# Gated cross-attention and gated feed-forward layer, one core: sums between the values of key tiles 0 and 1, probabilities of key tiles 1 and 3 in front of the values, correction and refinement in the values' slot, and a prologue that loads c and wk first

## The reference

```python
def _layernorm(x, axis=-1, eps=1e-05):
    m = jnp.mean(x, axis=axis, keepdims=True); v = jnp.var(x, axis=axis, keepdims=True)
    return (x - m) / jnp.sqrt(v + eps)
# attention: queries from the normalised x, keys and values from ctx
q = (Q @ Wq.T + bq) ...; k = (K @ Wk.T + bk) ...; v = (V @ Wv.T + bv) ...
scores = einsum('bhqd,bhkd->bhqk', q, k) * SCALE      # then key mask and causal mask
out = einsum('bhqk,bhkd->bhqd', softmax(scores), v)
x = x + tanh(g_xattn) * (out @ Wo.T + bo)
# feed-forward on the normalised x; xr, xk mix each token with the one before it
x = x + tanh(g_ffn) * (sigmoid(xr @ W_r.T) * (square(relu(xk @ W_k.T)) @ W_v.T))
```

## Time and profile before

| | us |
|---|---|
| median of 3 runs | 1927.38 |
| the profiled execution's own time | 1927.88 |
| its span, first to last instruction | 1926.1 |
| PE, DVE, POOL, ACT busy | 1873.3, 1292.7, 1204.3, 1086.5 |

### The profile page before, as it was taken

One profiled execution on the slowest core, in us unless ns is written; L12 is line 12 of the kernel. 1 busy time (PEld: TensorE's weight loads), 2 busy tenths in 40 slices (PEclk: granted clock), 3 DMA queues, 4 the chain that ended last, 5 costly groups with the idle time before them and its releaser, 6 DMA issues.

```text
span 1926.1 us, 35485 instructions
## 1 busy us (share of the span) xinstructions
PE 1873.3 (97%) x11136; PEld 1474.1 (77%) x11136; DVE 1292.7 (67%) x3656; ACT 1086.5 (56%) x2059; POOL 1204.3 (63%) x2001
## 2 busy tenths in 40 slices
PE   4899999999999999999999999998899999999999
PEld 3677777777777777777777777776678888888887
DVE  4767667677676776767776776777565756757653
ACT  4555555565555555555555555556655656656562
POOL 3577767777677777777777777776543423334331
PEclk9999999999999999999999999998999999999999
DMA  6454554545546455465455555563323232232311
GB/s 192 103 132 120 144 146 106 151 117 137 133 111 166 114 125 130 124 161 126 120 124 134 152 120 128 123 165 88 112 84 113 71 105 88 83 115 67 109 66 66
DMA packets 128697, 229.69 MB, mean 119 GB/s; under 512 B 18656, under 2 KB 20704, under 8 KB 127616
## 3 DMA queue, kind: packets, MB, share of 16 engines
q1 hardware_dynamic: 128512, 227.43, 44.3%
HBM read 92.06 MB, written 33.59 MB: 65 GB/s over the span
## 4 chain that ended last, share of the span: by engine, by line
PE 93%; DVE 2%; issue 1%; POOL 1%; ACT 1%; DMA 1%; SPq 0%; ACTq 0%; DVEq 0%; POOLq 0%
PE proj_ps L41 15%; PE proj_ps L42 15%; PE proj_ps L43 15%; PE score_ps L1243 10%; PE prob_ps L1267 8%; PE value_ps L1286 7%; PE score_ps L41 3%; PE score_ps L42 3%; PE score_ps L43 3%; PE sum_ps L1294 2%; PE sum_ps L42 1%; PE value_ps L42 1%; PE sum_ps L43 1%; PE sum_ps L41 1%; PE value_ps L43 1%; PE value_ps L41 1%
## 5 line engine op out<-in xcount | busy, mean ns | idle before, releaser
L965 DVE CUSTOM_DVE_ANT_0 score_ps<-score_ps,causal 128x128 f32<-128x128 f32 (+3 forms) x1024 | 487.2, 505 | 297.4 <-PE score_ps L1243 297.2
L620 ACT ACTIVATE probs<-prob_ps 128x512 f32<-128x512 f32 (+1 forms) x768 | 394.2, 527 | 365.6 <-PE prob_ps L1267 182.9
L1243 PE MATMUL score_ps<-k_stack,q_stack 97*128 97x128 f32 (+3 forms) x1024 | 316.2, 350 | 8.4 <-DVE least L965 4.4
L1267 PE MATMUL prob_ps<-q_stack,k_stack 100*128 100x512 f32 (+3 forms) x1024 | 281.5, 316 | 5.0 <-DMA q_stack<-max_rows 2.4
L452 POOL TENSOR_TENSOR prob_sum<-probs 128x384 f32<-128x384 f32 x256 | 259.5, 1014 | 0.0
L1243 PEld LDWEIGHTS score_ps<-k_stack,q_stack 97*128 97x128 f32 x1024 | 187.7, 189 | 79.2 <-issue 39.8
L501 POOL TENSOR_TENSOR kact<-square,kact 128x512 fp32r<-128x512 f32 x64 | 83.9, 1322 | 237.5 <-ACT kact L696 237.5
L455 POOL TENSOR_TENSOR prob_sum<-prob_sum,probs 128x256 f32<-128x256 f32 x256 | 194.4, 759 | 37.3 <-POOL prob_sum L452 0.9
L1267 PEld LDWEIGHTS prob_ps<-q_stack,k_stack 100*128 100x128 f32 x1024 | 191.8, 190 | 27.9 <-issue 5.5
L441 POOL TENSOR_SCALAR_AFFINE_SELECT probs<-probs 128x256 f32<-128x256 f32 x256 | 104.9, 410 | 152.5 <-ACT probs L620 152.5
L445 POOL TENSOR_SCALAR_AFFINE_SELECT probs<-probs 128x256 f32<-128x256 f32 x256 | 106.5, 416 | 105.2 <-ACT probs L620 105.2
(11 more groups left out here) (146 smaller groups left out, 4797.8 us busy)
## 6 DMA issues: line engine op xcount, KB each, us to landing
k_stack<-staged SPq DMA_DIRECT2D x384, 128.0 KB
q_stack<-staged SPq DMA_DIRECT2D x384, 128.0 KB, 3.1
tiles<-in_x SPq DMA_DIRECT2D x16, 1024.0 KB, 5.4
x_io<-in_x SPq DMA_DIRECT2D x16, 1024.0 KB, 7.9
x<-x_io SPq DMA_DIRECT2D x64, 256.0 KB, 3.1
res<-x SPq DMA_DIRECT2D x64, 256.0 KB, 3.7
out_x<-res SPq DMA_DIRECT2D x64, 256.0 KB, 2.0
tiles<-in_ctxT SPq DMA_DIRECT2D x60, 256.0 KB, 3.9
```

The costliest lines, as they stand in the source:

```text
L620: nc.scalar.activation(probs[:, u % RING, lo:hi], prob_ps[(3 * u + c) % 2][:, 0:hi - lo], ACT.Exp, scale=SCALE).then_inc(exp_done, 1)
L965: nc.vector.tensor_tensor_reduce(out=here, in0=here, in1=causal[:, LATE - P * t:S], scale=-1.0, scalar=3e38, op0=ALU.add, op1=ALU.min, acc ...
L1243: last = nc.tensor.matmul(here[:, at:at + P * (t + 1)], q_stack[n][0:MASK_ROW + 1, j, P * t:P * t + P], k_stack[n][0:MASK_ROW + 1, j, 0:P ...
L1267: last = nc.tensor.matmul(here[:, at:at + width], k_stack[n][0:ROWS, j, P * k:P * k + P], q_stack[n][0:ROWS, j, P * k:S], start=True, stop ...
```

## The change

1. **PE, values' slot.** `values` now computes key tile 0, then the sums, then key tiles 1 to 3. The sums report by `sums_done`, the values by `values_done`. Only the sums wait for POOL's `summed`; the values wait for `masked`. In slots that are multiples of 4 the probabilities' part 1 stands in front of the values.
2. **ACT.** Part 0 of the exponential and the logarithm wait for `sums_done` only; the inversion follows directly on the logarithm.
3. **DVE.** `correct` moves in front of the maximum over key range 2 of the same slot, `refine` from the next slot into this one, behind the last maximum. `normalise` also waits for `values_done`.
4. **Prologue.** Mask first, then c and wk in alternating quarters, x in quarters, bias columns, wq, wv, the mask's way back, wo, gates. The seed of 1 / sqrt(variance) is ACT's exp(-0.5 ln(.)) with one Newton step on DVE; DVE applies it. PE: k, four transposes, q 0, v 0, v 1, half of q 1. Weights are split in quarters; wo's low part goes over slots 1 and 2.

```diff
             def exponent(u, c):
-                    act.wait_ge(values_done, (u - RING) // HG + 1)
+                    act.wait_ge(sums_done if c == 0 else values_done, (u - RING) // HG + 1)
             def log_sums(G):
-                act.wait_ge(values_done, G + 1)
+                act.wait_ge(sums_done, G + 1)
# ACT, second(): behind log_sums; gone from third()
+                    invert_sums((i - VALUES) // HG)
# ACT, prologue
+            for k in range(K):
+                split_first_c(k)
+                split_weights("k", k)
+            act.wait_ge(columns_loaded, 16 * 3)
+            high_part_k(0, 0)
+            act.wait_ge(variance_ready, 1)
+            nc.scalar.activation(newton[:, 1, :], newton[:, 2, :], ACT.Ln).then_inc(variance_logged, 1)
+            act.wait_ge(variance_logged, 1)
+            nc.scalar.activation(newton[:, 1, :], newton[:, 1, :], ACT.Exp, scale=-0.5).then_inc(seed_ready, 1)
+            for m in range(T):
+                high_part_x(0, m)
+            for k in range(K):
+                split_weights("q", k)
...
# DVE, second()
-                if i % HG == 1 and 0 <= i - VALUES < N:
-                    refine((i - VALUES) // HG)
+                if i % HG == 0 and 0 <= i - VALUES < N:
+                    correct((i - VALUES) // HG)
# DVE, fourth()
-                    correct((i - VALUES) // HG)
+                    refine((i - VALUES) // HG)
# DVE, normalise
+                dve.wait_ge(values_done, G + 1)
# PE, values(G)
-                pe.wait_ge(summed, 3 * HG * (G + 1))
...
+                pe.wait_ge(masked, 2 * HG * (G + 1))
+                value_tiles(G, 0)
                 pe.wait_ge(max_copied, min(2 * G + 4, N // 2))
+                pe.wait_ge(summed, 3 * HG * (G + 1))
                 (the 8 matmuls of the sums)
+                last.then_inc(sums_done, 1)
+                for k in range(1, T):
+                    last = value_tiles(G, k)
                 last.then_inc(values_done, 1)
# PE, slot(i)
+                if then and i % HG == 0:
+                    probabilities(u, 1)
                 if i % HG == 0 and 0 <= i - VALUES < N:
                     values((i - VALUES) // HG)
...
-                if then:
+                if then and i % HG != 0:
                     probabilities(u, 1)
# SP, prologue
+            for k in range(K):
+                sp.dma_start(c_raw[:, k, :], ctxT[0, P * k:P * k + P]).then_inc(c_first_loaded[k], 16)
+                sp.dma_start(w_raw["k"][:, k, :], wkT[:, k, :]).then_inc(wk_first_loaded[k], 16)
+            for m in range(T):
+                sp.dma_start(tiles[:, m, :], x[0, P * m:P * m + P]).then_inc(x_first_loaded[m], 16)
```

More of the change, by code:

```diff
@@ L147, in gated_layer @@
         sum_ps = psum("sum_ps")
-        w_loaded = {n: sem(f"w{n}_loaded") for n in "qkvo"}
-        w_high, w_low = sem("w_high"), sem("w_low")
+        w_loaded = {n: sem(f"w{n}_loaded") for n in "qvo"}
+        w_high, w_low = ({n: sem(f"w{n}_{part}") for n in "qkvo"} for part in ("high", "low"))
         ffn_loaded = {n: sem(f"ffn_w{n}_loaded") for n in "krv"}
@@ L162, in gated_layer @@
         xt_done, xt_high, xt_low = sem("xt_done"), sem("xt_high"), sem("xt_low")
-        c_raw_loaded = sem("c_raw_loaded")
+        variance_ready, variance_logged, seed_ready, seed_step = (sem(f"first_{n}") for n in ("variance", "logged", "seed", "step"))
+        x_first_loaded = [sem(f"x_first_loaded{m}") for m in range(T)]
+        c_first_loaded = [sem(f"c_first_loaded{k}") for k in range(K)]
+        wk_first_loaded = [sem(f"wk_first_loaded{k}") for k in range(K)]
         c_loaded = [sem(f"c_loaded{k}") for k in range(K)]
@@ L537, in _ @@
                                     ALU.mult).then_inc(mask_scaled, 1)
+            pool.wait_ge(pool_const, 5)
+            pool.wait_ge(mask_scaled, 1)
+            for n, rows in enumerate((k_stack[0], q_stack[0], k_stack[1], q_stack[1])):
+                nc.gpsimd.memset(rows[MASK_ROW:P].bitcast(F32), 1.0).then_inc(stacks_set, 1)
+                pool.wait_ge(stacks_set, n + 1)
             pool.wait_ge(gate_ready, 1)
@@ L1122, in fourth @@
                     layernorm_stats(b + 1, 2)
-                if i == 1:
-                    split_weights(3, "o")
+                if i in (1, 2):
+                    for k in range(2):
+                        split_weights("o", 2 * (i - 1) + k)
                 if i == N - 9:
@@ L1155, in slot @@
                 fourth(i, b, s)
+            for k in range(K):
+                low_part_first_c(k)
+                split_weights("k", k)
             for m in range(T):
@@ L1235, in scores @@
                     pe.wait_ge(k_stacked[n][j // 2], k_stack_count(G))
+                if c == 0 and u in (0, HG):
+                    pe.wait_ge(stacks_set, (2, 4)[G])
                 if u > 0 or c == 2:
@@ L1295, in values, with value_tiles @@
                                             start=True, stop=True, skip_group_check=True)
+                last.then_inc(sums_done, 1)
+                for k in range(1, T):
+                    last = value_tiles(G, k)
                 last.then_inc(values_done, 1)
+            def value_tiles(G, k):
+                b, g = divmod(G, K)
+                for j in range(HG):
+                    at = P * (g % 2) + DH * j
+                    last = nc.tensor.matmul(value_ps[DH * j:DH * j + DH, P * k:S], v[:, value_block(b, g), k, at:at + DH],
+                                            probs[:, (HG * G + j) % RING, PT_AT[k]:PT_AT[k] + S - P * k],
+                                            start=(k == 0), stop=(k == T - 1), skip_group_check=True)
+                return last
             def free_bank(name, b):
```

152 lines of the change are left out of this document (80 added, 72 removed).

## The result

| | us |
|---|---|
| this kernel, median of 4 runs | 1943.42 (1943.25 to 1945.21) |
| the kernel before, median of 4 runs beside it | 1926.43 (1925.35 to 1927.60) |
| ratio, 95% interval | 1.0089, 1.0076 to 1.0101 |
| span of the profiled execution | 1941.5 (before: 1926.1) |

What follows compares the result with a forecast made beforehand. PE, busy 1873.3 of 1926.1 us, was taken as the bound. Span 1926.1 + 29.4 + 1.6 - 1.2 - 7 = 1948.9, then + 1.8 - 0.5 = 1950 us, 1.2% slower; range 1936 to 1958.

Steps and rivals of the forecast that it cites:

- The chain of the stall: Values' slot: sums, ACT's inversion, DVE's correction, maximum and its read in sequence make the next scores 0.72 us late.
- 0.64 us for each of 46 groups, +29.4 us: Values' slots with three projection products: 0.72 us stall plus 0.08 for weights, less 0.16 of vanished wait.
- The slots with six products, +1.6 us: In 16 slots three more projection products cover 0.69 of the 0.72 us stall, leaving 0.1 us each.
- only gain slack: Values' slot: while PE waits for the maximum's read, ACT and DVE gain slack and nothing else.
- The reorder on PE at 0: Values' slot: PE's new order of sums and values costs 0, bounds -0.1 to +0.1 us a group.
- The prologue, -7 us: Start of the kernel: first scores at 35 instead of 41.45 us, wo's split some 0.6 more; bounds -12 and 0.
- wq's low parts in parallel: Prologue: wq's low parts are made alongside x's transposes, high and low parts, which end at 20.5 us.
- the two ends for the q products: Prologue: 12 q products take 5.1 us at 0.43 each (counted) or 2.7 at 0.23, the two bounds.
- The end, -1.2 us: After the last values: earlier sums and 18 output products cover PE's 1.25 us wait; bounds 0 and -1.4.
- Rival (a): Values' slot: the correction finds its place, PE doesn't wait, 7.4 us come back, 1912 us; chance 0.09.
- Rival (d): Values' slot: inversion waits for all values, each of 46 stalls is 1.8 us, about 2003 us; chance 0.02.

Runs made afterwards that it cites:

- e4: The kernel before with DVE's move alone: correction in front of the 384-column maximum, refinement behind the last maximum; 2106.96 us, ratio 1.0924.
- e6: The changed kernel with ACT's inversion behind the exponential of part 1 again; 1991.77 us, ratio 1.0332.
- e5: e1 with the first normalisation of slots with s = 6 moved behind the exponentials of all three parts on ACT; 1909.99 us, ratio 0.9910.
- e1: The changed kernel with DVE's old order: correction behind the last maximum, refinement in the next slot; 1912.96 us, ratio 0.9924.
- e3: The changed prologue alone, with the slots of all engines in the order of the kernel before; 1920.77 us, ratio 0.9965.
- e8: e5 with c and wk of the first sequence loaded whole instead of in quarters; 1911.56 us, ratio 0.9920.
- e2: The changed kernel with the correction one place later, between the maxima over key ranges 2 and 3; 1913.99 us, ratio 0.9927.

## Why the prediction was right

Direction, mechanism and place were right; the loss forecast for the span, 22.8 us against 15.4, was half too large, by terms of both signs. Its steps, against the slot above:

- **The chain of the stall.** From the slot's start the prediction had exponential +2.91, logarithm +3.40, inversion +4.03, correction +4.71, maximum +5.32, end of the read +5.95. Measured: +2.95, +3.44, +4.07, +4.73, +5.34, +5.95. The one term off is from the read to the scores: 0.06 us, where I took 0.15 from an exponential's end. So the slot is 0.633 us longer, not 0.72.
- **0.64 us for each of 46 groups, +29.4 us.** +0.633 and then -0.060 (0.105 for weights that weren't loaded, less the waits around part 0 of the probabilities), 0.573 net: 26.4 us.
- **The slots with six products, +1.6 us.** 0.004 us each, 0.1 in all: with a stall of 0.63 the three more products of 0.69 hide it fully. In e4 and e6 slot 12 grew by 1.82 and 1.14, only 0.16 less than slots 0, 4 and 8. The cover is the same there, but ACT's list has a copy of c in front of the inversion in this slot, 0.51 us: 1.30 + 0.51 - 0.69 = 1.12, and 1.98 + 0.51 - 0.69 = 1.80. Timeline of ACT in slot 12 of e6:

```profile
697.99 0.61 ACT L619 CAST cT_high<-tiles 128x512 fp32r<-128x512 f32 x1
698.50 0.63 ACT L637 ACTIVATE inverse<-inverse 128x512 f32<-128x512 f32 x1
```

- **Slot 7, not foreseen.** 14 sequences x 0.30 = 4.3 us less. The prediction said that ACT and DVE "only gain slack", and took nothing from it; one wait of ACT for POOL still cost time in the old kernel, and the slack hid it. e5 shows that the same gain can be had without a stall.
- **The reorder on PE at 0.** e1, whose slots 0, 4 and 8 keep 5376 ns with the new order, shows 0.
- **The prologue, -7 us.** Slot 8, the first that has values, starts 5.8 us earlier, and with the old slots (e3) 6.2. The first k products and their 0.43 us pitch came as said, though PE waited 1.87 us for the second triple; of the first scores' -6.4 only -4.4 came (37.03 against 41.45). The step that failed is "wq's low parts in parallel": DVE made the last low part of x until 23.25 us, not 20.5, and only then the first of wq's, so the q products began at 23.99 and ended near 28.35, not at 26. Timeline of PE:

```profile
6.36 0.77 PE L41 MATMUL proj_ps<-cT_high,wk_high 128*128 128x512 f32 x1 [6.36 <-DVE wk_low L1034]
...
9.85 0.77 PE L41 MATMUL proj_ps<-cT_high,wk_high 128*128 128x512 f32 x1 [1.87 <-DVE wk_low L1034]
...
17.42 1.11 PE L1428 MATMUL proj_ps<-ident,tiles 128*128 128x128 f32 x4 [3.44 <-DVE tiles L1208]
...
23.99 0.77 PE L41 MATMUL proj_ps<-xT_high,wq_high 128*128 128x512 f32 x1 [2.09 <-DVE wq_low L1034]
...
37.03 0.58 PE L1293 MATMUL score_ps<-k_stack,q_stack 97*128 97x128 f32 x3
```

  Of the two ends for the q products (0.43 or 0.23 us each) the slow one was nearly right: behind the pauses of 3.44 and 2.09 us the first seven lie about 0.43 apart (24.99, 25.41, 25.84), the last four 0.23 (27.66, 27.90, 28.12). The rule cited there from the Trainium skill, "TensorE: Matmul & The Clock Gate", part 1, "The HAM clock gate", agrees with these starts. The rule on transfers of 1 MiB, cited from the Trainium skill, "DMA: Bandwidth & Descriptors", section "Bandwidth", is about throughput; for the start e8 is the test, and its whole transfers brought the first scores later and not earlier.

  One trace tells this term to about 1.5 us: in the seven traces with the new prologue slot 8 starts at 68.08 to 70.98 us, in the two with the old one (the old kernel and e4) at 75.82 and 77.06.
- **The end, -1.2 us.** The wait of 1.25 us for the last low part has gone, as said. But the attention's end did not get shorter. In slot 256 the sums also wait for ACT's copy of the maxima. Before, all values stood in front of them, and they waited 0.22 us; now only key tile 0 does:

```profile
1367.27 0.43 PE L1338 MATMUL sum_ps<-probs,ones 128*32 128x128 f32 x8 [1.95 <-ACT max_rows L613]
```

  e1 has the same 1.95 us, e3 with the old order has none. Counted from the start of slot 252, PE comes to the feed-forward's products behind the attention (1411.50 before, 1428.46 now) 1.1 us later than before, not 1.2 earlier: the sums' wait costs 1.7 against the 1.25 won, and about 0.6 had come up before slot 256. That the rest of the span still shows a gain of 0.5 us is luck: there the trace of the old kernel has nine products 0.43 us apart, and the changed one has none. Windows of the same work, before and now (the number behind POOL's count is the granted clock):

```profile
1411.40:1416.00 4.60, 4.50 (x13) 3.50 (x14) 1.29 (x2) 2.00 (x5) 1.27 (x1) 0.63 0.33 107
```

```profile
1428.40:1433.00 4.60, 4.54 (x24) 3.84 (x25) 1.99 (x3) 3.43 (x9) 1.29 (x1) 1.00 0.34 113
```

  That is 1.6 us, and it isn't the change's: e1 and e5 have such a stretch there (granted clock 0.65 and 0.64), e3 has not (1.00).

Sum of the terms as measured: 26.4 + 0.1 - 4.3 - 5.8 - 0.5 = 15.9 us; the spans differ by 15.4. Against the predicted 22.8 the difference is 3.0 from the size of the stall, 1.5 from slot 12, 4.3 from slot 7, less 1.2 and 0.7 at the two ends. The 0.7 is itself 2.3 of a wrong step, less the 1.6 of the clock.

Rival (a), no stall, is what e1 is: the read must come by the time at which the scores are due, and the correction in that place prevents it. Rival (d) is nearly e4: the inversion comes late, and the stall I priced at 1.8 us was 1.98. Its 2003 us would still have been too low where the clock falls, as e4's did.

## What to carry over

On an engine that is idle for microseconds, an instruction can still cost the bound engine its full time: ask what stands behind the one that waits, and which of those results the bound engine wants first. One place in the queue (e2) made the difference between 0.9% slower and 0.7% faster. After a change that adds a stall, look also at what the stall hides: a wait that vanished (slot 7) can be had for nothing. Work that is moved forward has less in front of it to hide its own waits (slot 256). And price a stall by its length: behind pauses of about 1.8 us TensorE's granted clock fell in e4 in 36 of 46 places, and a stall of 1.98 us cost 3.5.

## What the runs showed of the hardware

- In e4, a pause of TensorE of 1.83 us (recorded idle) at a granted clock of 1.00 was followed by 0.54 over the next 3.3 us (689.4 to 692.7). A loss of 1.5 us as there followed 36 of 46 such pauses and 6 of 15 pauses of 1.66 us; the rest cost nothing more. Pauses of 0.47 us (the changed kernel) and 1.14 us (e6), just as regular, left it at 1.00 from 116.9 to 1276.9 us.
- From the end of DVE's read of an accumulator to the matmul that it releases passed 0.06 us (613.90 to 613.96). The load of its weights started only then (613.96), that of the next matmul at 614.07; that matmul started 0.165 us behind the first, where it is 0.061 before (610.47 to 610.53).
